# Second-layer attention weights: made twice by matmul, the second time already transposed

## The reference

```
theta, phi, g = conv1x1(x)                      # each 128 x 1024 per image
attn = softmax(theta^T phi, axis=-1)            # 1024 x 1024
y = (attn @ g^T) reshaped to 128 x 1024
z = (1 - w) * x + w * conv1x1(y)
```

```
q, k = Wq z + bq, Wk z + bk                     # 16 x 1024 each
v = Wv z + bv                                   # 128 x 1024
att = softmax(q^T k / 4, axis=-1)               # 1024 x 1024
out = gamma * (v att^T)
result = Wf [out; z] + bf                       # 128 x 1024
```

## Time and profile before

| | |
|---|---|
| runs | 536.98, 537.65, 540.0 us, median 537.65 |
| profiled execution | 536.61 us, its span on the core 534.6 us |
| granted PE clock | 0.997 of full speed |
| busy: PE / DVE / ACT / POOL | 518.0 / 405.3 / 358.6 / 303.2 us |
| DMA | 15.24 MB, mean 29 GB/s |

### The profile page before, as it was taken

How to read it: one execution, slowest core, us unless ns; L and a number is a source line. 1 busy time by engine, 2 the same in 40 slices (tenths; PEclk the granted TensorE clock), 3 DMA queues, 4 the chain that set the end, 5 groups by cost and what they waited for, 6 DMA issues and landing times.

```text
span 534.6 us, 8449 instructions
## 1 busy us (share of the span) xinstructions
PE 518.0 (97%) x2933; PEld 438.2 (82%) x2933; DVE 405.3 (76%) x606; ACT 358.6 (67%) x652; POOL 303.2 (57%) x288
## 2 busy tenths in 40 slices
PE   8798999999999999999999999999999999899996
PEld 5677877888888888888888888888888888788886
DVE  5957686788677977778777887778867786888873
ACT  4564467657786577756877577765778656877763
POOL 1376365685267852877538753578536780274442
PEclk9899999999999999999999999999999999999999
DMA  5010000003000120002100020000300010001011
GB/s 183 15 40 2 0 16 0 2 2 106 9 0 21 40 67 9 20 1 67 40 10 21 0 99 16 1 21 1 105 9 1 20 42 27 9 1 34 2 41 39
DMA packets 6825, 15.24 MB, mean 29 GB/s; under 512 B 1280, under 2 KB 1792, under 8 KB 6784
## 3 DMA queue, kind: packets, MB, share of 16 engines
q1 hardware_dynamic: 6640, 14.57, 8.4%
q10 hardware_dynamic: 144, 0.13, 0.1%
HBM read 8.93 MB, written 4.19 MB: 25 GB/s over the span
## 4 chain that ended last, share of the span: by engine, by line
PE 91%; DVE 3%; ACT 3%; issue 1%; POOL 1%; DVEq 0%; ACTq 0%
PE trans L502 20%; PE accum L526 11%; PE accum L528 10%; PE accum L527 10%; PE scores L466 5%; PE scores L492 5%; PE scores L468 5%; PE scores L467 5%; PE misc L553 4%; PE misc L466 3%; PE misc L467 3%; PE misc L468 3%; PE misc L554 1%; PE misc L558 1%; ACT pt_hi L647 1%
## 5 line engine op out<-in xcount | busy, mean ns | idle before, releaser
L769 DVE TENSOR_TENSOR pt_lo<-trans,pt_hi 128x512 fp32r<-128x512 f32 x256 | 164.7, 685 | 67.5 <-ACT pt_hi L647 66.3
L647 ACT ACTIVATE pt_hi<-trans 128x512 fp32r<-128x512 f32 x256 | 138.8, 596 | 70.6 <-PE trans L502 69.0
L759 DVE TENSOR_REDUCE neg_max<-scores 128x1 f32<-128x1024 f32 x128 | 155.4, 1214 | 1.4 <-PE scores L468 1.4
L638 ACT ACTIVATE probs<-scores,neg_max 128x1024 f32<-128x1024 f32 x128 | 143.9, 1124 | 6.8 <-DVE neg_max L759 6.8
L502 PE MATMUL trans<-ident,probs 128*128 128x128 f32 x1024 | 134.4, 274 | 2.4 <-ACT probs L638 2.4
L502 PEld LDWEIGHTS trans<-ident,probs 128*128 128x128 f32 x1024 | 116.3, 141 | 13.6 <-ACT probs L638 3.8
L526 PE MATMUL accum<-pt_hi,g_hi 128*128 128x512 f32 x136 | 54.4, 400 | 0.0
L528 PE MATMUL accum<-pt_hi,g_lo 128*128 128x512 f32 x136 | 53.4, 393 | 0.0
L527 PE MATMUL accum<-pt_lo,g_hi 128*128 128x512 f32 x136 | 53.4, 392 | 0.0
L466 PE MATMUL scores<-phi_hi,theta_hi 128*128 128x512 f32 x112 | 48.9, 437 | 0.2 <-POOL phi_lo L880 0.2
L867 POOL TENSOR_TENSOR theta_hi<-proj_full,zero 128x512 fp32r<-128x512 f32 x14 | 14.6, 1040 | 59.0 <-ACT proj_full L666 59.0
(11 more groups left out here) (145 smaller groups left out, 992.0 us busy)
## 6 DMA issues: line engine op xcount, KB each, us to landing
x_keep<-x_dram SPq DMA_DIRECT2D x8, 512.0 KB, 3.3
out_dram<-o_sb SPq DMA_DIRECT2D x15, 256.0 KB, 2.5
x_raw<-x_tiles_dram SPq DMA_DIRECT2D x7, 512.0 KB, 3.6
k_op<-qk_op SPq DMA_DIRECT2D x16, 96.0 KB, 2.3
x_raw<-x_tiles_dram SPq DMA_DIRECT2D x2, 256.0 KB, 3.2
w_all<-weights_t_dram SPq DMA_DIRECT2D x1, 336.0 KB, 3.8
out_dram<-o_sb SPq DMA_DIRECT2D x2, 128.0 KB, 1.9
w_all<-weights_t_dram ACTq DMA_DIRECT2D x1, 128.0 KB, 3.2
```

What stands on the lines that cost most here:

```text
L638: nc.scalar.activation(probs[:, k % 2, :], scores[:, k % 2, :], ACT.Exp, bias=neg_max[:, k % 4:k % 4 + 1], accum_out=row_sum[:, slot(gb), ...
L647: nc.scalar.activation(pt_hi[:, gb % 2, 4 * bank:4 * bank + 4, t * P:(t + 1) * P], trans[:, cols(bank)].rearrange("p (n q) -> p n q", n=4) ...
L759: nc.vector.tensor_reduce(neg_max[:, k % 4:k % 4 + 1], scores[:, k % 2, :], AX.X, ALU.max, negate=True).then_inc(max_ready, 1)
L769: nc.vector.tensor_tensor(pt_lo[at], trans[:, cols(bank)].rearrange("p (n q) -> p n q", n=4), f(pt_hi[at]), ALU.subtract).then_inc(pt_lo_r ...
```

## The change

Layer 1 stays as it is. In layer 2:

- A unit still makes its scores, maximum and exponentials (now over its scores in PSUM, `result = scores[...]`), but only the row sums are kept. `pair_log` takes log(sum) on ACT for two units at a time, `split_shift` on POOL makes shift = -max - log(sum) and splits it in hi and lo, and SP writes these to a small DRAM tensor (`turned`, 4-byte pieces) and reads them back as two rows of the stacked q operand, rows 48 and 49 (`shift_in`). The k operand holds ones in those rows (`clear_keys`), so a score matmul adds the shift.
- Late scores: at the steps in `LATE_STEPS` (4gb+9 to 4gb+12 for block gb, later or closer at the end) PE makes the scores again with the operands exchanged, k tile against all 512 queries, two matmuls a piece, four pieces a block, into `trans`. ACT's exponential of it (128x1024, into one of three SBUF tiles `fulls`) is the normalised weight, already transposed. POOL copies it rounded into `pt_hi` (`late_hi`), DVE subtracts into `pt_lo` (`late_lo`).
- The transposes, evictions and subtractions of layer-2 units, the r groups, the diagonals, `r_rows`, the multiplication by it and POOL's addition go; DVE's drain now is `accum` + f.
- Layer 2's value chunks move from 4gb+6 to 4gb+14; the last block's from steps 128 to 131 to steps 134 to 137. Layer 1's stay. The last block is no longer split in pairs.
- POOL rounds with `tensor_copy` instead of an addition of zero. The loop is written out. The ACT table set is asked for at the start. The last image keeps its q and k in theta's and phi's tiles; more buffers for v and f.

```diff
+LATE_STEPS = {gb: tuple(TPB * gb + 9 + j for j in range(CPB)) for gb in range(len(BLOCKS)) if BLOCKS[gb][0] == 1}
+LATE_STEPS.update({24: (109, 110, 111, 112), 27: (116, 117, 118, 119), 28: (120, 121, 122, 123),
+                   29: (124, 125, 126, 127), 30: (128, 129, 130, 131), 31: (132, 133, 134, 135)})
+VALUE_STEPS = [tuple(TPB * gb + (14 if BLOCKS[gb][0] else 6) + c for c in range(CPB)) for gb in range(len(BLOCKS))]
+VALUE_STEPS[24], VALUE_STEPS[27], VALUE_STEPS[28] = (114, 115, 116, 117), (118, 119, 120, 121), (122, 123, 124, 125)
+VALUE_STEPS[29], VALUE_STEPS[30], VALUE_STEPS[31] = (126, 127, 128, 129), (130, 131, 132, 133), (134, 135, 136, 137)
...
# SP
+                        if k == TPB * gb + 3 + 2 * pair:
+                            sp.wait_ge(shift_split, 3 * pairs(gb, pair))
+                            sp.dma_start(rows[pair].rearrange("r t p -> p (r t)"), shift_parts[:, h, pair, :, :].rearrange("p r t -> p (r t)"),
+                                         allow_slow_non_contiguous=True).then_inc(shift_out[pair], 16)
+                    if k == TPB * gb + 7:
+                        for pair in range(2):
+                            sp.wait_ge(shift_out[pair], 16 * (LATE.index(gb) + 1))
+                        sp.dma_start(f(qk_of(b)[3 * CK:3 * CK + 2, cols(h)]).rearrange("r (q c) -> r q c", q=2),
+                                     rows.rearrange("q r t p -> r q (t p)")).then_inc(shift_in[h], 16)
...
# PE
+            def late_scores(gb, j):
+                _, b, h = BLOCKS[gb]
+                pe.wait_ge(shift_in[h], 16 * (b + 1))
+                for bank in range(2):
+                    trans_free(("late", gb, j), bank)
+                    tile = slice((2 * j + bank) * P, (2 * j + bank + 1) * P)
+                    last = nc.tensor.matmul(trans[:, cols(bank)], k_of(b)[:, tile], qk_of(b)[:, cols(h)],
+                                            start=True, stop=True)
+                last.then_inc(late_scores_ready, 1)
...
                 for group in after:
-                    small(group, it)
-                if 0 <= k - 1 < UNITS:
-                    unit_transposes(k - 1, it)
+                    small(group)
+                for gb, j in late_fills(k):
+                    late_scores(gb, j)
+                if 0 <= k - 1 < UNITS and (k - 1) // TPB in FIRST:
+                    unit_transposes(k - 1)
...
# ACT
+            nc.scalar.preload_act_table_set("natural_log_exp_and_others")
...
+            def pair_log(gb, pair):
+                at = slice(2 * pair, 2 * pair + 2)
+                act.wait_ge(probs_ready, units(TPB * gb + 2 * pair + 1))
...
+                nc.scalar.activation(log_sum[:, BLOCKS[gb][2], at], row_sum[:, slot(gb), at], ACT.Ln).then_inc(log_ready, 1)
...
+            def late_exp(gb, j):
+                act.wait_ge(late_scores_ready, late(gb, j))
+                full_free(act, ("late", gb, j))
+                nc.scalar.activation(fulls[:, full_of(("late", gb, j)), :], trans[:, :], ACT.Exp).then_inc(late_ready, 1)
...
+                for gb, j in late_fills(k - 1):
+                    late_exp(gb, j)
+                if 0 <= k - 2 < UNITS and (k - 2) // TPB in FIRST:
+                    unit_hi(k - 2)
                 if 0 <= k - 1 < UNITS:
-                    unit_exp(k - 1, it)
+                    unit_exp(k - 1)
+                    gb, t = divmod(k - 1, TPB)
+                    if gb in LATE and t % 2:
+                        pair_log(gb, t // 2)
...
# DVE
+            def clear_keys(keys, n):
+                nc.vector.memset(keys[:, :].bitcast(f32), 0.0).then_inc(k_cleared, 1)
+                dve.wait_ge(k_cleared, 2 * n + 1)
+                nc.vector.memset(keys[2 * CK:4 * CK, :].bitcast(f32), 1.0).then_inc(k_cleared, 1)
...
+            def late_lo(gb, j):
+                dve.wait_ge(late_hi_ready, late(gb, j))
+                if j == 0:
+                    side_free(dve, gb)
+                at = (slice(None), side(gb), slice(2 * j, 2 * j + 2), slice(0, HALF))
+                nc.vector.tensor_tensor(pt_lo[at], fulls[:, full_of(("late", gb, j)), :].rearrange("p (n q) -> p n q", n=2),
+                                        f(pt_hi[at]), ALU.subtract).then_inc(late_lo_ready, 1)
...
+                if k == TPB * FIRST[-1] + TPB + 2:
+                    dve.wait_ge(scores_ready, units(TPB * FIRST[-1] + TPB - 1))
+                    clear_keys(k_of(B - 1), 2)
                 before, after = SCHEDULE[k]
                 for group in before:
-                    small(group, it)
+                    small(group)
                 if 0 <= k < UNITS:
-                    unit_max(k, it)
+                    unit_max(k)
+                for gb, j in late_fills(k - 1):
+                    late_lo(gb, j)
...
# POOL
             def round_to(hi, full):
-                return nc.gpsimd.tensor_tensor(hi, full, zero[:, :].broadcast_to([P, full.shape[1]]), ALU.add)
+                return nc.gpsimd.tensor_copy(hi, full)
...
+            def late_hi(gb, j):
+                pool.wait_ge(late_ready, late(gb, j))
+                if j == 0:
+                    side_free(pool, gb)
+                nc.gpsimd.tensor_copy(pt_hi[:, side(gb), 2 * j:2 * j + 2, :].rearrange("p n q -> p (n q)"),
+                                      fulls[:, full_of(("late", gb, j)), :]).then_inc(late_hi_ready, 1)
...
                 if k in SPLIT_X:
-                    split_x(SPLIT_X[k], it)
...
+                    split_x(SPLIT_X[k])
+                for gb in LATE:
+                    for pair in range(2):
+                        if k == TPB * gb + 3 + 2 * pair:
+                            split_shift(gb, pair)
+                for gb, j in late_fills(k - 1):
+                    late_hi(gb, j)
                 for group in SCHEDULE[k][0] + SCHEDULE[k][1]:
-                    small(group, it)
```

More of the change, by code:

```diff
@@ L641, in unit_hi @@
-            def unit_hi(k, it):
+                act.wait_ge(max_ready, units(k))
+                if gb in FIRST:
+                    full_free(act, ("first", k))
+                    if t == 0 and sums(gb) > 2:
+                        act.wait_ge(r_inv_ready, sums(gb) - 2)
+                    result = fulls[:, full_of(("first", k)), :]
+                else:
+                    if t == 0 and pairs(gb, 0) > 4:
+                        act.wait_ge(log_ready, pairs(gb, 0) - 3)
+                    result = scores[:, k % 2, :]
```

505 lines of the change are left out of this document (239 added, 266 removed).

## The result

The changed kernel takes 562.3 us (median of 559.87, 560.83, 563.76, 565.28) against 538.71 for the kernel before in the same session: ratio 1.0455, 95% interval 1.0425 to 1.0484. It is 4.5% slower, and 21 us over the 541 forecast, outside the range. The profiled execution is the one of 560.83, with a span of 559.0. Ratios and intervals here leave out executions that lie over 1.5% above the fastest of the same kernel, which matters for two experiments (e4 and e15). (A word in the description of the kernel before is wrong: the five periods from step 20 on are a loop only in the Python that writes the program. Both programs are straight lines, of 8449 and 7609 instructions, so writing the loop out changes nothing on the chip.)

The account below looks back on a forecast made before the run. PE was taken to bound the middle, queues and the late chain the end. Span 534.6 + 2.0 - 6.5 - 4 x 2.2 - 2.7 - 2.0 + 19.2, plus 3 for late copies, plus 2.0 outside: 541 us, range 529 to 552.

Parts of the forecast that it names:

- The way of the shift row: Row out to DRAM and back: each transfer some 2.6 us, within some 11 us at block 31.
- A late score that waits for a DMA: Sign, at layer 2's late score matmuls, that the prediction is wrong altogether; no size given.
- the shift row or the logs: Rival: piecewise row transfer 10 us longer delays the end's blocks, 550 and over, or table reloads, 556; chance together 0.1.
- The tables: Part of a rival: ScalarE reloads its table for every log, 82 us, giving 556; chance 0.1 together with the row.
- The run-out: Step 128 to the end: chain of late scores and drains makes 31.0 us from 11.81, +19.2.
- Steps 100 to 127: Two stretches: 100 to 116 shrinks 2.7 despite key clearing, 117 to 127 shrinks 2.0.
- The middle: Each 16-step period: PE work 59.0 plus waits 1.1 and 0.9 makes 61.1, -2.2.
- the drain (forecast 0.9): Step 6 of a period: PE waits for VectorE's drain of accum, +0.9.
- v's quarter ahead of y: Step 0 of a period: PE waits to start y for v's last quarter behind the late subtraction, +1.1.
- Ahead of the middle: Start of the kernel: memsets +2.0, later steps up to the middle -6.5.
- The port: Rival: GpSimd and VectorE shut each other out of SBUF in late copies and subtractions, 550; chance 0.25.
- PE stays the bound: Rival: the waits of steps 0 and 6 in a period don't come, giving 527; chance 0.25.

Follow-up runs that it names:

- e4: Changed kernel with the rounded late weight made by a second ScalarE exponential instead of GpSimd's 64 copies: ratio 1.0496.
- e15: Changed kernel with only the run-out mended (value chunks of blocks 29 to 31 three steps behind, a second bank to gather in): 552.6 us.
- e14: Changed kernel with the row written in 16-byte pieces and gathered back, its transfers ahead of SyncE's key copy, fetch one step earlier: 547.2 us.
- e2: Changed kernel with the shift row written in 128 pieces of 16 bytes, wrong order, late exponential scaled by 0.001: 550.9 us.
- e5: Changed kernel with the row written in 16-byte pieces and fetched in right order by two transfers gathering 4-byte pieces: 559.9 us.
- e8: Changed kernel with the gathered row of e5, all key tiles cleared by GpSimd and the run-out mended: 549.0 us.
- e9: e8 with SyncE issuing the row's transfers ahead of the key copy, and the fetch one step earlier: 535.5 us.
- e13: Changed kernel, slow row write kept, with SyncE issuing the row's transfers ahead of the key copy of that step: 556.7 us.
- e7: Changed kernel with the gathered row of e5, first key tiles and the last image's key tile cleared by GpSimd: 553.0 us.
- e10: e9 with VectorE draining the small groups ahead of the late subtraction in steps 108 to 119: 533.6 us.
- e16: e10 with VectorE's small groups ahead of its late subtraction from step 20 on: 529.65 us, ratio 0.9873.
- e1: Separate program timing single VectorE and GpSimd operations alone and side by side, and small transfers: eight pairs side by side take 15.9 us.
- e12: Changed kernel with an extra GpSimd copy of 928 columns out of SBUF behind each of the 64 late copies: 590.8 us.
- e3: Changed kernel with the two key tiles cleared by GpSimd at its start instead of by VectorE in step 2: 561.0 us.
- e11: The memset twin of e12: changed kernel with an extra GpSimd memset of 928 columns behind each of the 64 late copies: 558.8 us.

## Why the prediction was wrong, step by step

**The way of the shift row: the step that failed.** It said that "each some 2.6 us by today's small one" and that "there are some 11 us" of room, so it cost nothing. Two things were wrong. The size: a write in 4-byte pieces takes 8.6 us in the kernel and 9 to 11 alone; the row I took it from moves another shape the other way. And the place: I counted the transfers' durations and not what the fetch stands behind in SyncE's queue, the key copy, which itself waits for a drain. Mending both brings the time to 547.2 (e14), 15.1 us less and inside the range; the order alone gives 5.6, the quick write with a gathered fetch 2.4, and the quick write with the plain fetch 11.4 (e2, whose row is in the wrong order). These are differences to the one session of the changed kernel. Free of it are the 12.7 and 13.5 us that the order gives once the write is quick (e5 to e14, e8 to e9). "A late score that waits for a DMA" was in my list of signs that the prediction is wrong altogether, and after has six such waits, 5.4 us. The rival "the shift row or the logs" had this direction, with 10 us more, and I gave it 0.1 together with the tables; it should have had far more, because the one row it rested on was of another kind. The tables were right: one load. (No step of the prediction leads from the 82 us to the 556 that it gives for them.)

**The clock behind the waits: a term put at nothing.** In the changed kernel the waits for the row are only a part of what it costs. From unit 100 to the end PE is idle for 25.8 us in after and 24.2 in e14, but busy for 117.3 and 110.2 us with the same 508 matmuls, at a mean granted clock of 0.93 and 0.99. So 7.1 of the 8.7 us between the two in this stretch is time at the lower clock, for which the sum had no term. Why the clock fell behind one wait and not behind another is not shown: the wait of 1.84 us before 514.54 in after is followed by a stretch at 1.2 GHz, the one of 1.85 before 505.26 in e14 is not.

**The run-out: +19.2 forecast, +22.9 measured.** The mechanism (two steps per trip through ScalarE, GpSimd, VectorE; drains that hold first chunks) is what PE's timeline of after shows:

```profile
532.15 0.47 PE L529 MATMUL accum<-pt_hi,g_hi 128*128 128x512 f32 x1 [2.25 <-DVE o_sb L860]
...
538.76 0.50 PE L529 MATMUL accum<-pt_hi,g_hi 128*128 128x512 f32 x1 [1.12 <-DVE pt_lo L801]
```

The first is block 30's first chunk behind the drain, 2.25 us and not the 0.7 of the drain by itself, because the drain stands in VectorE's queue behind a late subtraction. Between them PE ran part of the time at the lower clock (0.90 in this window), which the sum did not have. With the row mended (e14) the window is

```profile
514.73:545.25 30.52, 19.71 (x76) 13.24 (x75) 12.92 (x12) 9.61 (x12) 11.05 (x12) 1.00 0.09 27
```

30.5 us, +19.6 over before where I had +19.2: the same 76 matmuls take 19.7 us instead of 22.6, and PE's idle time is 10.8 instead of 11.2. So the mechanism and its size were right, and the rest is the lower clock. It goes with the slow row in these traces: in the run-outs of after, e13 and e15 the clock is 0.89 to 0.95, with the quick row (e2, e5, e14) 1.00. That I took this schedule as given was no error, but it was not needed: its mend is worth 3 to 5 us (e15, e8).

**Steps 100 to 127: -4.7 forecast, +6.2 measured.** The 1.9 us of clearing in VectorE's queue do show, as PE's wait of 2.6 for y. Costed as growth by 0.8, they were too small. But taking them away moved the time by 0.2 only (e7), as the row was waited for behind them. With order and row mended, 100 to 127 takes 103.8 us (e14), before 103.0, after 109.2. So up to 5.4 of the 10.9 that were off is the row's, 4.1 of it busy time at the lower clock; the rest is v's quarter, y and the drains, each behind a late subtraction. e10 and e16 take part of these away.

**The middle: -2.2 a period forecast, -1.06 measured.** I added up, over one period of after (312 to 374.4), what PE's starts lie apart beyond the unhindered spacing (0.233 us behind a matmul of 512 columns). That gives 2.1 us of stalls, where I had 2.0, but others: 0.8 for the drain (forecast 0.9), 0.4 for v's quarter ahead of y (forecast 1.1), 0.6 for an eviction on ScalarE and 0.3 for the row (not forecast). PE's own work fell by 3.6 and not 4.3: a step lost its transposes and their price, but the 0.09 us by which the matmul behind them starts late turned up elsewhere, in front of value chunks. The rest, 0.4 a period, is not settled: with a quick row the four periods take 247.3, with the slow one 249.0 (after) and 249.5 (e13), but 247.5 in e15, whose program is that of after there.

**Ahead of the middle: -4.5 forecast, -0.5 measured.** The memsets cost 2.3 between units 0 and 4 (forecast 2.0). The rest is mostly this one execution: its first exponential starts at 15.04, those of all experiments at 12.4 to 13.3. In e15, the same program up to there, unit 36 starts at 163.4, 4.0 ahead of before and near the 4.5 that I had.

**The port: forecast as a rival at 0.25, +3 in the sum.** The two shut each other out (e1), and the marks are in after: subtractions 1.32 instead of 1.22 (eleven of 64 last 1.6 to 2.1), `x_lo` 3.02 where it took 2.40 in the twin with the memset. It also reaches the row. A subtraction of two elements on GpSimd, 0.2 us alone, meets a late subtraction of VectorE (526.36 to 527.59) and lasts 1.00:

```profile
526.63 1.00 POOL L954 TENSOR_TENSOR shift<-neg_max,log_sum 128x2 f32<-128x2 f32 x1 [0.31 <-ACT log_sum L652]
527.70 0.18 POOL L957 CAST shift_parts<-shift 128x2 fp32r<-128x2 f32 x1
```

Its share of the end time is not shown: the memset twin, with hardly any of it, is 3.5 us quicker in spite of 56 us more on GpSimd, so neither the 3 that I put in nor the 12 of the rival is ruled out by it. But with the port untouched e14 comes to 547.2, so the port is not what put the time outside the range. By the Trainium skill, SBUF — State Buffer, section Who interferes with whom, the two shut each other out for whole instructions. The trace of e1 agrees (1.98 us from pair to pair, where alone they start 1.15 and 0.99 apart), and what it costs depends on where they meet: 32 us with one more reading copy in the wrong place (e12).

**PE stays the bound** (527): not as written. With the queues in order the kernel comes to 529.65, near that number, but by way of a mended head and run-out, so it does not confirm the rival's sum.

What stays open: the port's share, and how much of the 21 us missing belongs to the one session and not to the kernel, since e15's trace is 6.4 us ahead of after's in the part that they share. What has to happen for PE's clock to fall is open too.

## What to carry to other kernels

When a change adds a small transfer, write down what stands ahead of it in the issuing queue and what that waits for: a late place and a long duration hide each other, and mending one can show little. Price a transfer from one with the same piece size and direction. And when an edit gives nothing, look for the late thing behind it: here the head's 6.7 us appeared only once the row's write was quick. Add up an engine's busy time beside its waits, since a wait can also cost clock.

## What the runs showed of the hardware that was not expected

- A DMA out of SBUF in 512 pieces of 4 bytes took 9.0 to 11.3 us alone and 8.6 in the kernel; the same 2 KB in 16-byte pieces 1.4 to 2.3, and 512 pieces of 4 bytes read from DRAM 2.1 to 2.3.
- GpSimd's copy of 1024 fp32 elements out of SBUF and VectorE's subtraction of two SBUF tiles run nearly in turn (1.04 and 1.22 alone, 2.04 and 1.95 side by side); with two inputs on both, 3.4 and 3.2 each. GpSimd's subtraction of two elements, 0.2 alone, took 1.00 in 7 of 32 cases in after, each beside such a subtraction of VectorE.
- GpSimd's `memset` of 1024 columns takes 0.95 us (e3) where VectorE's takes 0.91, and VectorE's subtractions stay at 1.23 us with 64 such memsets of 928 columns in the run (e11).
- What a lower granted clock of TensorE can cost: from unit 100 to the end the same 508 matmuls were 117.3 us of busy time at a mean of 0.93 (after) and 110.2 at 0.99 (e14).
